# Tap weights of a small attention chain: nine matmuls of 8 rows become one of 72 rows on a masked vector, and the gelu of levels 2 and 3 is issued before the features

## What is computed

```python
def _conv_att2(x, kg_w1, kg_b1, kg_w2, kg_b2, lk_filter, fus_w, fus_b):
    b = x.shape[0]
    f_att, f_idt = (x[:, :ATT], x[:, ATT:])
    pooled = f_att.mean(axis=(2, 3))
    hdn = jax.nn.gelu(pooled @ kg_w1.T + kg_b1, approximate=False)
    ker = (hdn @ kg_w2.T + kg_b2).reshape(b, ATT, 1, SK, SK)
    ...
    out_dk = jax.vmap(dyn)(f_att, ker)
    out_lk = _conv(f_att, lk_filter, pad=LK // 2)
    out = jnp.concatenate([out_lk + out_dk, f_idt], axis=1)
    return _conv1x1(out, fus_w, fus_b)
```

## Time and profile before

| | us |
|---|---|
| median of 3 runs | 2907.32 (2903.9 to 2908.01) |
| the profiled execution, whole | 2903.58 |
| its span in the profile | 2901.8 |
| PE busy | 2649.9 (91% of the span) |
| DVE busy | 2140.3 (74%) |
| ACT busy | 1054.7 (36%) |
| POOL busy | 627.5 (22%) |
| mean granted TensorE clock | 0.943 of full speed |

### The profile page before, as it was taken

How to read it: one execution, slowest core, us unless ns; L and a number is a source line. 1 busy time by engine, 2 the same in 40 slices (tenths; PEclk the granted TensorE clock), 3 DMA queues, 4 the chain that set the end, 5 groups by cost and what they waited for, 6 DMA issues and landing times. The chain is left out here.

```text
span 2901.8 us, 38918 instructions
## 1 busy us (share of the span) xinstructions
PE 2649.9 (91%) x12262; PEld 2127.6 (73%) x12262; DVE 2140.3 (74%) x2968; ACT 1054.7 (36%) x1641; POOL 627.5 (22%) x663
## 2 busy tenths in 40 slices
PE   5899999987999699999999698999966999999998
PEld 4677777766888588888887577777755777777776
DVE  5444444454454688888888889999877999999998
ACT  1211111111100588999898322222203333233232
POOL 6544443403220444444443100000001000000000
PEclk9999999997988799999999799999977999999999
DMA  7222222201000777777776223333443333333342
GB/s 148 62 74 70 68 71 71 64 17 37 13 13 8 161 220 218 219 219 215 216 215 173 95 103 149 148 134 134 153 172 111 94 106 108 92 116 99 94 122 58
DMA packets 288702, 338.04 MB, mean 116 GB/s; under 512 B 24816, under 2 KB 243824, under 8 KB 274288
## 3 DMA queue, kind: packets, MB, share of 16 engines
q1 hardware_dynamic: 280736, 334.74, 39.2%
q10 hardware_dynamic: 7888, 2.29, 0.5%
HBM read 211.60 MB, written 122.62 MB: 115 GB/s over the span
## 5 line engine op out<-in xcount | busy, mean ns | idle before, releaser
L168 PE MATMUL ps_all<-vh,u_h 128*128 128x512 f32 x960 | 385.0, 401 | 28.3 <-DVE vl L2818 27.4
L170 PE MATMUL ps_all<-vh,u_l 128*128 128x512 f32 x960 | 383.6, 400 | 0.0
L169 PE MATMUL ps_all<-vl,u_h 128*128 128x512 f32 x960 | 383.1, 399 | 0.0
L2727 ACT ACTIVATE vh<-rt,gn 128x528 fp32r<-128x528 f32 x192 | 130.4, 727 | 446.1 <-DVE rt L2795 314.6
L168 PE MATMUL ps_all<-vh,t_h 128*128 128x512 f32 x576 | 231.2, 401 | 23.7 <-DVE vl L1873 23.7
L168 PEld LDWEIGHTS ps_all<-vh,u_h 128*128 128x128 f32 x960 | 181.0, 189 | 81.9 <-issue 35.4
L169 PE MATMUL ps_all<-vl,t_h 128*128 128x512 f32 x576 | 230.0, 399 | 0.0
L170 PE MATMUL ps_all<-vh,t_l 128*128 128x512 f32 x576 | 229.2, 398 | 0.0
L170 PEld LDWEIGHTS ps_all<-vh,u_l 128*128 128x128 f32 x960 | 181.1, 189 | 46.3
L169 PEld LDWEIGHTS ps_all<-vl,u_h 128*128 128x128 f32 x960 | 181.3, 189 | 45.5
L1712 POOL TENSOR_TENSOR zr<-zr,z 128x256 f32<-128x256 f32 x128 | 122.5, 977 | 342.8 <-DMA xr<-in_x 342.8
(11 more groups left out here) (401 smaller groups left out, 6733.5 us busy)
## 6 DMA issues: line engine op xcount, KB each, us to landing
xr<-in_x SPq DMA_DIRECT2D x128, 256.0 KB, 3.6
x_layer<-xr SPq DMA_DIRECT2D x64, 512.0 KB, 2.7
xq<-x_layer SPq DMA_DIRECT2D x32, 1024.0 KB, 4.9
x_layer<-xq SPq DMA_DIRECT2D x32, 1024.0 KB, 3.8
out<-ot SPq DMA_DIRECT2D x64, 512.0 KB, 5.2
xw<-in_x SPq DMA_DIRECT2D x112, 288.0 KB, 4.3
xc<-in_x SPq DMA_DIRECT2D x120, 256.0 KB, 3.9
xw<-x_layer SPq DMA_DIRECT2D x16, 1152.0 KB, 8.7
```

Of the source, the lines that this page charges most:

```text
L168: pe.matmul(o, wh, xh, start=first, stop=False, skip_group_check=True)
L169: pe.matmul(o, wh, xl, start=False, stop=False, skip_group_check=True)
L170: return pe.matmul(o, wl, xh, start=False, stop=last, skip_group_check=True)
L2727: act.activation(vh[:, v % 2, n, :, :].rearrange("p a b -> p (a b)"), rt[:, n, :, :].rearrange("p a b -> p (a b)"), ACT.Identity, scale=gn ...
```

## The change

The hidden vector is now made nine times over: `kg1` has 72 columns (column 9h + t is hidden row h, for t from 0 to 8), so `chain_hidden` gives 72 rows, the gelu works on 72 partitions, and `kb1` has 72 rows. A new operation on DVE, `chain_blocks_dve`, multiplies these 72 values with a mask `tapeye` of 72 x 9, whose row 9h + t is 1 in column t and 0 elsewhere; the result `hdt` has 9 blocks of columns, and block t holds the hidden vector in the rows of tap t alone. One matmul of 72 rows against `hdt` then gives all taps at once. A new semaphore `blk` tells PE that `hdt` is there.

DVE does the new operation after the chunks in level 1, before `features(g, 0)` in levels 2 and 3, and after the copies of the base filter in level 0. In levels 2 and 3, `chain_act` on ACT now stands before `features(g, 0)` instead of behind it. The loads at the start get longer: `kg1` is loaded nine times into every ninth column, and `kb1` and `tapeye` with eight DMAs each.

```diff
-        kg1 = mb("kg1", [ATT, ATT // 2])
-        kb1 = mb("kb1", [ATT // 2, 1])
-        kg2 = mb("kg2", [ATT // 2, 9, P])
+        kg1 = mb("kg1", [ATT, NH * 9])
+        kb1 = mb("kb1", [NH * 9, 1])
+        kg2 = mb("kg2", [NH * 9, P])
+        tapeye = mb("tapeye", [NH * 9, 9])
...
-            pe.matmul(ps_chain[0:ATT // 2, 8:8 + n], kg1[:, :], pooled[:, 0:n], start=True, stop=True,
+            pe.matmul(ps_chain[0:NH * 9, 8:8 + n], kg1[:, :], pooled[:, 0:n], start=True, stop=True,
                       skip_group_check=True).then_inc(s_chain, 1)
...
-            pe.wait_ge(s_hdn, image + 1)
-            for t in range(9):
-                mm = pe.matmul(ps_chain[:, 16 + n * t:16 + n * t + n], kg2[:, t, :], hdn[:, 0:n],
-                               start=(t == 0), stop=True, skip_group_check=True)
-            mm.then_inc(s_chain, 1)
+        def chain_taps(pe, image, n, s_blk, s_chain):
+
+            pe.wait_ge(s_blk, image + 1)
+            pe.matmul(ps_chain[:, 16:16 + 9 * n], kg2[:, :], hdt[:, 0:9 * n], start=True, stop=True,
+                      skip_group_check=True).then_inc(s_chain, 1)
+
+        def chain_blocks_dve(dve, image, n, s_hdn, s_blk):
+
+            dve.wait_ge(s_hdn, image + 1)
+            dve.tensor_tensor(hdt[:, 0:9 * n].rearrange("p (t k) -> p t k", k=n),
+                              hdn[:, 0:n].unsqueeze(1).to_broadcast([NH * 9, 9, n]),
+                              tapeye[:, :].unsqueeze(2).to_broadcast([NH * 9, 9, n]), ALU.mult).then_inc(s_blk, 1)
...
-            late = [(kg1[:, :], kgw1t), (kb1[:, :], kgb1.rearrange("(c a) -> c a", a=1)),
-                    (tapm[:, :, :], tapmask), (chm[:, :], chmask)]
+            late = [(kg1[:, t::9], kgw1t) for t in range(9)]
+            late += [(tapm[:, :, :], tapmask), (chm[:, :], chmask)]
...
-                late += [(kg2[:, :, sp16], kgw2)]
+                late += [(kg2[:, sp16], kgw2.rearrange("h t c -> (h t) c"))]
+                late += [(kb1[9 * q:9 * q + 9, :], kgb1[q:q + 1].unsqueeze(0).to_broadcast([9, 1])),
+                         (tapeye[9 * q:9 * q + 9, :], chmask[0:9, 0:9])]
...
                             for c in range(NX - 3, NX):
                                 prep_chunk(i + 1, c)
+                        chain_blocks_dve(dve, i, 1, hdn_s, blk_s)
...
                         act.wait_ge(zero, NZ)
+                        chain_act(act, g, NI1, chain, hdn_s)
                         features(g, 0)
-                        chain_act(act, g, NI1, chain, hdn_s)
                         features(g, 1)
...
+                        chain_blocks_dve(dve, g, NI1, hdn_s, blk_s)
                         features(g, 0)
```

More of the change, by code:

```diff
@@ L30 @@
 NI = C - ATT
+NH = ATT // 2
 LK = 13
@@ L155, in conv_kernel @@
         wrs, bb = mb("wrs", [P, 10]), mb("bb", [P, 8])
-        hdn = mb("hdn", [ATT // 2, 4])
+        hdn = mb("hdn", [NH * 9, 4])
+        hdt = mb("hdt", [NH * 9, 9 * 4])
         cst = ctx.enter_context(ExitStack())
@@ L283, in chain_act @@
             act.wait_ge(s_chain, 3 * image + 2)
-            act.activation(hdn[:, 0:n], ps_chain[0:ATT // 2, 8:8 + n], ACT.Gelu, bias=kb1[:, 0:1]).then_inc(s_hdn, 1)
+            act.activation(hdn[:, 0:n], ps_chain[0:NH * 9, 8:8 + n], ACT.Gelu, bias=kb1[:, 0:1]).then_inc(s_hdn, 1)
         def shift_tap(sh, sw):
@@ L460, in conv_kernel @@
             pooled_s, chain, hdn_s, ker_s = s1("pooled"), s1("chain"), s1("hdn"), s1("ker")
+            blk_s = s1("blk")
             dyn = Steps(s1("dyn"), DSTEPS)
@@ L1016, in body @@
                         between = {4: lambda: chain_hidden(pe, i, 1, 1, pooled_s, chain),
-                                   10: lambda: chain_taps(pe, i, 1, hdn_s, chain),
+                                   10: lambda: chain_taps(pe, i, 1, blk_s, chain),
                                    NSTAT: lambda: dyn.at(pe, i, DSTEPS)}
@@ L1565, in body @@
                         pointwise(g, 0)
-                        chain_taps(pe, g, NI1, hdn_s, chain)
+                        chain_taps(pe, g, NI1, blk_s, chain)
                         pointwise(g, 1)
@@ L1581, in conv_kernel @@
         pooled = mb("pooled_all", [ATT, B])
-        hdn = mb("hdn_all", [ATT // 2, B])
+        hdn = mb("hdn_all", [NH * 9, B])
+        hdt = mb("hdt_all", [NH * 9, 9 * B])
         rs = mb("rs0", [P, B, NPAIR // 8])
@@ L2039, in conv_kernel @@
             t_s, t_h, t_k, t_p, t_c = sl("t_s"), sl("t_h"), sl("t_k"), sl("t_p"), sl("t_c")
+            t_b = sl("t_b")
             t_r = Steps(t_s, 1)
@@ L2496, in _ @@
                         b_s.done(dve.tensor_copy(wf[:, cb, 2:5, :], base))
+                    chain_blocks_dve(dve, 0, B, t_h, t_b)
                     b_s.wait(dve)
@@ L2586, in _ @@
                     chain_hidden(pe, 0, B, 1, t_p, t_c)
-                    chain_taps(pe, 0, B, t_h, t_c)
+                    chain_taps(pe, 0, B, t_b, t_c)
                     b_s.at(pe, 0, NBS)
```

1 line of the change is left out of this document (removed).

## The result

The changed kernel takes 2888.6 us (median of four runs, 2885.2 to 2889.7), the kernel before 2907.6 beside it: a ratio of 0.9937, with a 95% interval of 0.9925 to 0.9949. A second set gave 2888.4 us and 0.9944 (0.9931 to 0.9957). The forecast was 2889.9.

The account below looks back on a forecast made before the run. The prediction took level 1 to be bound by PE's own work plus short handovers. Its terms, -15.0 - 13.2 + 0.2 + 10.6 = -17.4 us, took 2907.3 to 2889.9 us, range 2880 to 2897.

Parts of the forecast that it names:

- Level 1: Taps on PE in eight images: two passes in place of eighteen, less a wider hidden matmul; -15.0 us.
- the new wait: Level 1, PE waiting for DVE's masked multiplication: ready 2.1 us ahead of PE, so it costs nothing.
- Rival C: Level 1 gives nothing because the last chunk's load comes late and PE waits for the mask; 2904.9 us, 6%.
- Levels 2 and 3: Second pointwise part on PE starts earlier, 3.4 us for each of four groups less 0.10; -13.2 us.
- The engine named as next in line: Levels 2 and 3: the second pointwise part waits for DVE's L1369, ending at 693.25, and starts at 693.30.
- Rival B: Levels 2 and 3 give nothing because something behind the pointwise part does not move with it; 2903.1 us, 8%.
- The start: 23 more DMAs on SP delay the second image's chunks and PE's work from there on; +10.6 us.
- 23 x 0.647 = 14.9 for the list: SP's list of loads at the start: 23 more DMAs at the mean issue price, 14.9 us.
- the slack between the landing of the chunk and POOL's start: At the start, 1.35 us between a chunk's landing and POOL starting on it, taken off the longer list's cost.
- Rival A: The longer list of loads at the start is hidden, leaving only the gains of 28.0 us; 2879.3 us, 9%.
- Rival D: Slower: SP's issues at the start cost more than 0.65 us each; at 1.8 us, +9.2 and 2916.5 us, 3%.
- Level 0: Fewer passes give nothing as PE waits for DVE; the multiplication goes into DVE's late queue, +0.2 us.

Follow-up runs that it names:

- the runs on both sides of it: 23 more loads on the kernel before: 2919.0 us, ratio 1.0043; the changed kernel with 6 loads instead of 35: 2878.2 us, ratio 0.9898.
- the last run above: Kernel before with the gelu of levels 2 and 3 moved ahead and DVE's masked multiplication added into an unread tile: 2907.7 us, ratio 1.0002.

## Why the prediction was right

The forecast, 2889.9, is 1.3 us from the median. The terms were less exact than the sum: by the medians the change gave 19.0 us where 17.4 were forecast, and by the spans of the two profiles 13.9. An agreement to 1.3 us is finer than these runs can show, and some of it is luck. (The chances given for faster add up to 0.90, not 0.89.)

**Level 1** (forecast -15.0). Sixteen passes fewer, at 0.11 to 0.12 us each. Measured across the taps 2.47 - 0.42 = 2.05 us in place of 1.97, and 0.09 us for the wider hidden matmul in place of 0.10. That gives 1.96 an image; the seven periods in the trace came to 1.83 and, in the second profile, 2.07 each. Issuing the matmuls nine times over in this level cost 15 to 16.5 us. The term was right, and so was its reason why the new wait would cost nothing: in image 1, the one of the earlier trace rows, the mask was ready 1.95 us ahead of the taps, where 2.1 was forecast, and in the other images 1.9 to 4.4 us ahead. The multiplication itself took 0.50 us there and not 0.22. Rival C is out.

**Levels 2 and 3** (forecast -13.2). 12.2 us in the trace, 11.6 in the second one. The engine named as next in line, DVE with `fjl`, is the one, at all four groups. The forecast had it end at 693.25 and PE start 0.05 us behind; the handover was 688.32 - 688.18 = 0.14 us, and ACT and DVE started on the features 0.42 and 0.75 us after the last row of the pointwise part, where it was 0.36 and 0.69 before. Where the sizes differ between groups, so does the clock: 2.92 us at a granted clock of 1.00 from the hidden matmul to the end of the first pointwise part, 3.4 to 3.6 where it was 0.73 to 0.75, and 4.26 (second group of the second profile) where it was 0.50. Rival B is out: these levels' nine matmuls cost 10.3 us when issued again.

**The start** (forecast +10.6, measured +7.8; the term that was mis-sized). Two steps of it failed, in opposite directions. First, 23 x 0.647 = 14.9 for the list, which became only 10.3 us longer (54.37 to 65.23, of which 0.56 is SP's later arrival). The eight more loads of `kg1` took their 0.64 us each. But the fifteen others, of `kb1` and `tapeye`, took 0.41 on average (0.36 for most) and not 0.65, which is 3.6 us. And the change also reshaped the eight loads of `kg2`, from 8 x 9 x 16 to 72 x 16: seven of them went from 0.73 to between 0.36 and 0.49 us, and the eighth took 2.04, so that together they gave back 1.1; the prediction counted the new DMAs and left the reshaped ones as they were. In the run with the loads alone, the list grew by 14.5 us, so near to 14.9 partly by luck: it has one issue of 2.40 in it, and the other small loads took 0.49 on average.

Second, the slack between the landing of the chunk and POOL's start was there in the kernel before (1.1 us, where the forecast had 1.35 from the median landing of all 120 loads of `xc`), but it was used up. These are DVE and POOL before, then DVE with the change (POOL's row at 71.07 stands above):

```profile
61.93 1.29 DVE L734 BATCH_NORM_STATS2 stat<-xc 128x6 f32<-128x512 f32 x2
62.02 1.09 POOL L589 TENSOR_TENSOR rl<-rf,rh 128x512 fp32r<-128x512 f32 x1 [1.29 <-DVE rh L858]
```

```profile
70.92 1.29 DVE L745 BATCH_NORM_STATS2 stat<-xc 128x6 f32<-128x512 f32 x2 [9.08 <-DMA xc<-in_x]
```

Before, DVE had the chunk at 61.93, and POOL took it at 63.07, right behind `rl`. A chunk comes in two loads, issued half a microsecond apart, and their landings took 3.6 and 4.1 us. With the change they took 4.5 and 5.1, and both engines stood waiting for them. What differs is what SP does next: before, it issued two loads and had to wait for a buffer until about 60.8; with the change both buffers were free when it came to them, and four loads went out in a row. In all fourteen profiles the second load landed after 4.1 to 4.5 us where two went out (six profiles) and after 5.0 to 5.9 where four did (eight). That the two loads behind slow down the two ahead fits this; no run tested it by itself. So the issue moved by 65.34 - 57.27 = 8.07 us, the chunk on DVE by 8.99, and POOL, whose slack took up the difference, by 8.00. The 2.9 us of idle time was right, and so was the path behind it: PE's last plain part moved by 8.14. Rival A is out, by the runs on both sides of it.

The Trainium skill, "DMA: Bandwidth & Descriptors", section "Anatomy of one DMA — SWDGE (gpsimd) path", gives about 50 ns of dispatch for DMAs that GpSimd issues; the shortest issue that I found on SP is 0.27 us and most are 0.32 to 0.64, so its price doesn't carry over to this queue. Of the Trainium skill's rule on the same page, section "Rules for kernel authors", against a strided last dimension: the nine loads with `kg1[:, t::9]` took 0.64 us each and the one contiguous load of the same operand 0.63 to the start of the next; no engine waited for either. For pieces this small the rule made no difference here. Rival D is out: in the whole list one load took over 1.4 us to issue, 2.00, and no other did.

**Level 0** (forecast +0.2). The multiplication there took 0.23 us. But the stretch from `rsum_all` to the end became 2.6 to 3.1 us longer, and that was in no term: the prediction put everything behind level 0's chain at nothing. It lies against the 2.8 us by which the start was cheaper than forecast. That the two cancel is luck, and it is the reason why the sum was better than its terms.

The stretches of the profiles side by side, in us (the changed kernel in both of its profiles):

| from | to | before | changed | difference |
|---|---|---|---|---|
| PE's first matmul | large filter, image 0 | 60.1 | 67.9, 68.1 | +7.9 |
| large filter, image 0 | large filter, image 7 | 528.0 | 515.2, 513.5 | -13.7 |
| large filter, image 7 | PE's first matmul of level 0 | 356.1 | 342.5, 343.5 | -13.0 |
| PE's first matmul of level 0 | `rsum_all` | 629.7 | 630.8, 630.2 | +0.8 |
| `rsum_all` | end | 1300.5 | 1303.6, 1303.1 | +2.9 |

They sum to -15.1; the medians are 17.7 us apart in one set and 19.0 in the other. The profiled execution of the kernel before was 4.0 us under its median (2903.6 against 2907.6), which makes up for the difference in size; in which stretch those 4 us would lie, one profile can't tell.

## What to carry to other kernels

Small matmuls on a path are priced by the pass. With weights of 128 columns a pass took 0.11 to 0.12 us at 2.4 GHz and 0.22 at 1.2, with 8 rows or 72 and with 1 to 36 columns of data; making the weights of the hidden matmul 72 columns wide in place of 8 cost 0.09 us for two. So nine that share a vector are worth folding into one, even if another engine must first spread that vector out. Before such a change is priced as a gain, look where its extra loads stand: put them behind the transfers that the next stage waits for, or fetch them in one piece; here that was worth 7 to 10 us, a third to a half of what the change itself gave. And count the DMAs whose shape changes along with the new ones.

## What was unexpected of the hardware

With one more multiplication on DVE in each block of the program's earlier stages, a stretch of 720 us at the end, in which no instruction is changed, is longer: 722.1 to 722.4 us in the eleven profiles that have it, 720.7 to 720.9 in the three that don't. In one of the eleven nobody reads its result. The addresses of the tiles were excluded, the mechanism was not found.

The issue of a DMA on SP took from 0.3 to 0.7 us by its shape. In each of the eight kernels whose list of small loads was still running then, a single issue at 55 to 57 us took 1.3 to 2.8 us, whatever its shape; the row of 2.00 us above is one. Why is open.

DVE's masked multiplication took from 0.17 to 0.66 us, with a median of 0.50:

```profile
L272 DVE TENSOR_TENSOR hdt<-hdn,tapeye x12: 166/496/659, 103.1 to 876.5; 72x9 f32<-72x9 f32 x8, 72x36 f32<-72x36 f32 x4
```

The bias of the taps, with as many columns, took 0.17 us at nearly all its places in the kernel before:

```profile
L279 DVE TENSOR_TENSOR kerr<-ps_all,kb x12: 168/169/196, 99.7 to 898.0; 128x9 f32<-128x9 f32 x8, 128x36 f32<-128x36 f32 x4
```

The difference is not in the shape but in what POOL does at the time. In level 1 and in levels 2 and 3:

```profile
102.85 0.74 POOL L320 TENSOR_TENSOR pl<-pl,xc 128x256 f32<-128x256 f32 x1 [0.18 <-POOL pl L317]
103.12 0.50 DVE L272 TENSOR_TENSOR hdt<-hdn,tapeye 72x9 f32<-72x9 f32 x1
...
747.68 2.47 POOL L1233 TENSOR_TENSOR rl<-rfb,rh 128x512 fp32r<-128x512 f32 x1 [13.33 <-DVE rh L1370]
749.55 0.65 DVE L272 TENSOR_TENSOR hdt<-hdn,tapeye 72x36 f32<-72x36 f32 x1 [0.37 <-ACT hdn L292]
```

In ten of the twelve places the multiplication started while POOL was in an operation, and in all ten it ended 0.02 to 0.05 us after that operation. In the other two, with POOL idle as it started, it took 0.17 and 0.19. With 8 rows in place of 72 (the last run above) it was the same: 0.49 to 0.75 behind a running operation of POOL, 0.16 and 0.18 without. The bias, which reads one of its operands from `ps_all`, took 0.17 at 99.69, in the middle of an operation of POOL from 99.26 to 100.56. Nobody waited for these tenths of a microsecond here.
